# Two pieces of TensorE work put ahead of the scores, and two pieces of VectorE work put ahead of their neighbours

## The chip, the core and the metric

The kernel runs on one core of a Trainium2 chip. Its metric is device time in microseconds (us). Before the change: 723.44 us, the median of three runs (723.38 to 723.95).

## The reference

What is computed, shortened (B = 64 batches of S = 32 rows, D = 256; context of 257 rows of 192; 16 heads of 16; 8 experts):

```python
# 1. cross attention with a residual
xn = layernorm(x);  q = xn @ Wq;  k = ctx @ Wk;  v = ctx @ Wv        # 16 heads of 16
attn = softmax(q k^T / 4 + mask) over the 257 context rows
x  = x + (attn v) @ Wo
# 2. local attention, window of 2 rows to each side, with a residual
xn = layernorm(x);  Q = xn@Wq2+bq;  K = xn@Wk2+bk;  V = xn@Wv2+bv
x  = x + softmax(Q K^T / 16 inside the window) V
# 3. a top-1 router over 8 experts, three layers each, with a residual
xn = layernorm(x);  e = argmax(xn @ Wr + br)
h = gelu(xn@W1[e]+b1[e]);  h = gelu(h@W2[e]+b2[e]);  x = x + h@W3[e]+b3[e]
```

## The kernel before, in words

**Stages.** The first 409 us compute the two attentions and the router's logits, the rest routes the 2048 rows to slots of 128 and runs the experts. The change lies in the attention stage alone.

**Tiles and steps.** A tile T is 128 rows, four batches of 32; there are 16 tiles. Each engine (TensorE, VectorE, ScalarE, GpSimd and the DMA queue SP) has a program of its own, an iteration over T in which k runs from 0 to 3. One pair (T, k), a *step*, is one batch of cross attention, n = 4T + k, and a part of the work on finished tiles. Iterations T = -1, 0, 1 and 14, 15 are written out, 2 to 13 are a hardware loop, and a `last_tile()` closes the stage. The order of each engine's work is the order of its program: nothing overtakes. The engines meet only at semaphores, which are waited for as counts.

**TensorE in one step** (names used below, with the lines of the kernel): **scores** (L1442, function `scores`) of batch n into four banks `ps_s`; **weigh** (L1456), the probabilities of batch n-1 times its values into `ps_o`; **keys** (L1423) of batch n+1 into `ps_kv`; the **first turn** (L1470, `transpose_probs(n, 0)`), the first 128 columns of the probabilities transposed in four pieces into `ps_p`, each piece after ScalarE's exponentials of it; **values** (L1431) of batch n+1, after ScalarE has copied the keys out of `ps_kv` (L819); the **second turn** (L1470 again, `transpose_probs(n, 1)`) into the same bank `ps_p`, for which VectorE must have copied the first turn out (`p_copied[0]`). So the second turn waits for VectorE's copy in every step.

**Between them stands the work on older tiles**, all of it through one bank, `ps_m`, whose users take turns by the semaphores `m_filled` and `m_emptied` (functions `turn` and `my_turn`). At k = 0 the next rows are turned (L1515) and the queries made (L1524). At k = 1 the **output product** (L1579, `end(T, 1)`): `attnT` times Wo for tile T-1; and the local probabilities times their values for tile T-2 (L1487). At k = 2 the **turn of rows** (L1494, `middle(T, 2)`), which transposes `xn2`, the normalised rows of tile T-1; then queries and keys of local attention (L1583). At k = 3 local scores (L1505) and local values (L1497).

**VectorE in one step.** The **masks** (L1040): four instructions, one for each bank of scores, which add the mask, write `prob` and give the row's minimum, the exponential's bias. Then, by k: at k = 1 the **residual** x2 (L1149) and its statistics (L1024, L1027, function `add_input`); `finish_batch` (L1050, L1053, L1057) for batch n-1, whose last instruction writes `attn`; at k = 1 the local result x3 (L1111, L1084); the **copy of the probabilities** (L1062, `copy_probT`, 128x512), which releases the second turn; and `end(T, k)`. In `end(T, 0)` the tile's attention is turned (L1157) and the last context row's value is added (L1160), which gives `attnT`, the operand of the output product at k = 1. In `end(T, 1)` the statistics of x3 are taken (`moments_of(2, ...)`, L1024 and L1027), and x2 is normalised into `xn2` (`normalise(1, ...)`, L1031), the operand of the turn of rows at k = 2.

**ScalarE and GpSimd.** ScalarE makes the four exponentials (L815), copies keys and values out of `ps_kv` (L819, L823), rounds the context (L810) and copies the second turn out (L827). GpSimd keeps the last probability (L657), makes each 1/sqrt(variance) (L663, L665), splits the context into two parts (`split_ctx`, L644, 128x512, both inputs in SBUF), places the queries (L649), and shifts the context (`shift_ctx`, L637, 128x512).

Of the kernel before, what the change touches and what calls it, by code (L numbers as in the profile page):

```python
# [20 lines left out]
def perceiver_kernel(nc, x, ctx_turned, last_turned, mask, Wq, Wk, Wv, Wo, lWq_turned, lbq, lWk_turned, lbk, lWv, lWv_turned, lbv,  # L21
# [32 lines left out]
    with ExitStack() as stack:  # L54
# [103 lines left out]
        x2 = passing("x2", [P, D])  # L158
        x2_kept = passing("x2_kept", [P, D])
        xn2 = sb("xn2", [P, D])  # L160
# [240 lines left out]
        def in_tiles(T):  # L401
            return not isinstance(T, int) or 0 <= T < TILES
# [609 lines left out]
        def _(dve):  # L1012
# [140 lines left out]
            def end(T, k):  # L1153
                has_q, has_out, has_local = parts(T)
                if k == 0 and has_out:
                    dve.wait_ge(o_done, BT * T)
                    d.transpose(attn_turned[:, :, :, :].rearrange("p b c s -> p (b c s)"),  # L1157
                                attn[:, :, :].rearrange("p b d -> p (b d)")).then_inc(attn_turned_done, 1)
                    dve.wait_ge(attn_turned_done, T)
                    d.tensor_tensor(attnT[:, :, :].rearrange("p c (b s) -> p c b s", b=BT),  # L1160
                                    attn_turned[:, :, :, :].rearrange("p b c s -> p c b s"),
                                    last_vT[:, :, bass.ds(BT * (T - 1), BT)].unsqueeze(3).to_broadcast([P, 2, BT, S]),
                                    ALU.add).then_inc(attnT_done, 1)
                if k == 1 and has_local:
                    dve.wait_ge(x3_done, T - 1)
                    moments_of(2, T - 2, x3n[:, 0:D])
                if k == 1 and has_out:
                    normalise(1, T - 1, x2[:, :], xn2[:, :], xn2_done)
                if k == 2 and has_out:
                    dve.wait_ge(m_filled, turn(T, 5) + 1)  # L1170
                    d.tensor_tensor(lqk[:, 0:2, :], ps_m[:, 0:2 * P].rearrange("p (w s) -> p w s", w=2),
                                    lq_bias[:, :].unsqueeze(2).to_broadcast([P, 2, P]), ALU.add).then_inc(m_emptied, 1)
                if k == 3 and has_out:
                    dve.wait_ge(band_done, T)
                    alone(dve)
                    mask_local_scores(ps_m[:, 3 * P:3 * P + S]).then_inc(m_emptied, 1)
# [7 lines left out]
            def iteration(T):  # L1184
                has_q, has_out, has_local = parts(T)
                first = isinstance(T, int) and T < 0
                if first:
                    dve.wait_ge(x_in, 16)
                    moments_of(0, 0, xt[:, :])
                    dve.wait_ge(mask_bytes_in, 16)  # L1190
                    d.tensor_scalar(mask_rows[:, :], mask_bytes[:, :], 1.0, -MASKED, ALU.subtract, ALU.mult).then_inc(mask_done, 1)
                    normalise(0, 0, xt[:, :], xn1[:, :], xn1_done)
                    dve.wait_ge(wk_rounded, 1)
                    split_first_rows(0, wk_split)
                    middle(T, 0)
                    split_last_rows(0, wk_split)
                    dve.wait_ge(wv_rounded, 1)
                    split_first_rows(1, wv_split)
                    split_last_rows(1, wv_split)
                    return  # L1200
                for k in range(BT):
                    n = BT * T + k
                    opening = isinstance(T, int) and T == 0 and k == 0
                    if opening:
                        dve.wait_ge(x_in, 32)
                        moments_of(0, 1, xt[:, :])
                    if k == 1 and has_local:
                        dve.wait_ge(lexp_done, T - 1)
                        d.reciprocal(lrow_inv[:, :], lrow_sum[:, :]).then_inc(linv_done, 1)
                    at = 3 if opening else 2  # L1210
                    if in_tiles(T):
                        mask_scores(T, n, k, range(at))
                    if k == 2:
                        middle(T, k)
                    if opening:
                        normalise(0, 1, xt[:, :], xn1[:, :], xn1_done)
                    if in_tiles(T):
                        mask_scores(T, n, k, range(at, GROUPS))
                    if k == 0:
                        middle(T, k)  # L1220
                    if k == 2 and has_local:
                        normalise(2, T - 2, x3n[:, 0:D], x3n[:, D:2 * D], xn3_done)
                        scale_logits(T - 2).then_inc(logits_done, 1)
                    if k == 1 and has_out:
                        add_input(T)
                    if k == 1 and isinstance(T, int) and T == 1:
                        fuse_router()
                    if isinstance(T, int) and T == 0 and k == 0:
                        last_rows()
                    if not first and exists(T, k - 1) and not (isinstance(T, int) and BT * T + k > B):  # L1230
                        finish_batch(T if k else T - 1, (k - 1) % BT)
                    if k == 3 and next_rows(T):
                        dve.wait_ge(x_in, 16 * (T + 3))
                        moments_of(0, T + 2, xt[:, :])
                    if k % 2:
                        middle(T, k)
                    if in_tiles(T):
                        copy_probT(n)
                    if k == 3 and next_rows(T):
                        normalise(0, T + 2, xt[:, :], xn1[:, :], xn1_done)  # L1240
                    end(T, k)
                    if isinstance(T, int) and T == 0 and k >= 2:
                        fuse_local_weights(k)

# [136 lines left out]
            k = 0  # L1381
# [32 lines left out]
        def _(pe):  # L1414
# [181 lines left out]
            def iteration(T):  # L1596
# [13 lines left out]
                for k in range(BT):  # L1610
                    n = BT * T + k
                    ahead = in_tiles(T) and exists(T, k + 1)
                    has_q, has_out, has_local = parts(T)
                    if in_tiles(T):
                        scores(n, k)
                    if k == 0 and has_q and not (isinstance(T, int) and T == 0):
                        turn_next_rows(T)
                    opening = isinstance(T, int) and T == 0
                    if opening and k in (1, 2):
                        fuse_weights(k - 1)  # L1620
                    if opening and k == 3:
                        fuse_bias(0, 1, 0)
                    if k == 1:
                        end(T, k)
                    if k == 2:
                        middle(T, k)
                    if isinstance(T, int) and T == 0 and k == 0:
                        pe.wait_ge(wv_split, 2)
                        values(0, 0)
                        last_rows()  # L1630
                    if isinstance(T, int) and T == 0 and k == 1:
                        pe.wait_ge(last_copied, 1)
                    if k == 3 and has_out:
                        my_turn(T, 6)
                        local_scores(ps_m[:, 3 * P:3 * P + S]).then_inc(m_filled, 1)
                    if exists(T, k - 1) and not (isinstance(T, int) and BT * T + k > B):
                        weigh(T if k else T - 1, (k - 1) % BT)
                    if ahead:
                        keys(n + 1, (k + 1) % 2)
                    if k == 0 and isinstance(T, int) and T == 0:  # L1640
                        turn_next_rows(T)
                    if k % 2:
                        middle(T, k)
                    if k == 1 and isinstance(T, int) and T == 1:
                        fuse_router()
                    if k == 2:
                        end(T, k)
                    if opening and k == 3:
                        fuse_bias(2, 0, 2)
                        fuse_biases()  # L1650
                    if in_tiles(T):
                        transpose_probs(n, 0)
                    if k == 0 and has_q:
                        queries(T)
                    if ahead:
                        values(n + 1, (k + 1) % 2)
                    if in_tiles(T):
                        transpose_probs(n, 1)
# [254 lines left out]
```

## Time and profile before

| what | value |
|---|---|
| runs | 723.38, 723.44, 723.95 us |
| the profiled execution | 723.63 us, span of its instructions 721.9 us |
| TensorE (matmul) busy | 695.3 us, 96% of the span |
| TensorE weight load busy | 586.4 us, 81% |
| VectorE, ScalarE, GpSimd busy | 469.1 us, 451.1 us, 425.4 us |
| granted TensorE clock over the span | 0.986 of full speed |
| attention stage, 180 to 220 us | TensorE 40.00 of 40 us, VectorE 27.86, ScalarE 26.77, GpSimd 24.30; clock 1.00 |

A matmul's busy time runs until its modelled end, which overlaps the next one's start, so 40.00 of 40 us does not say that nothing waits. The weight loads (PEld in the rows) don't overlap each other, and their starts are the better clock of TensorE's progress. Idle time is in square brackets behind a row, with what ended it; "issue" is a gap that no semaphore explains. Within the loop a tile takes 24.5 us, again and again the same to a few hundredths.

### The profile page before, as it was taken

The numbers are of one execution on the slowest core, as the hardware profiler recorded it, in microseconds if no ns is written. First come the engines' busy times: TensorE is split into PE (matmuls) and PEld (weight loads), VectorE is DVE, ScalarE is ACT, GpSimd is POOL, SyncE is SP. The second block draws the span as 40 slices with busy tenths as digits, with TensorE's granted clock in tenths as the row PEclk, the third lists the DMA queues.
The fourth block names the chain that finished last, engine by engine and source line by source line (L and its number), as shares of the span: only waits on it lengthen the run. The fifth ranks groups of instructions, "written<-read, shape, count | busy, mean of one in ns | idle before, by whom it ended". The sixth has DMA issues, their size and how long they took to land.

```text
span 721.9 us, 26603 instructions
## 1 busy us (share of the span) xinstructions
PE 695.3 (96%) x9305; PEld 586.4 (81%) x9306; DVE 469.1 (65%) x1416; ACT 451.1 (62%) x1073; POOL 425.4 (59%) x578
## 2 busy tenths in 40 slices
PE   8999999999999999999999848999999999999996
PEld 7888888888888888888888737888888888888885
DVE  4466777777777766777777669999952990268000
ACT  4656666666666666666666344575756666575754
POOL 6476565656565656556665114677766676767553
PEclk9999999999999999999999978999999999999999
DMA  7433233322333343434322904239033531271000
GB/s 213 113 86 83 68 82 97 88 80 75 97 92 80 80 95 82 93 80 95 88 80 79 372 31 161 96 98 316 23 103 117 190 118 45 83 237 58 30 7 1
DMA packets 55985, 74.21 MB, mean 103 GB/s; under 512 B 6557, under 2 KB 41662, under 8 KB 55936
## 3 DMA queue, kind: packets, MB, share of 16 engines
q1 hardware_dynamic: 49792, 60.63, 29.7%
q0 software_dynamic: 2944, 8.13, 3.5%
q10 hardware_dynamic: 3200, 4.80, 1.8%
q8 instruction: 30, 0.49, 0.3%
q14 instruction: 19, 0.16, 0.1%
HBM read 67.17 MB, written 7.27 MB: 103 GB/s over the span
## 4 chain that ended last, share of the span: by engine, by line
PE 91%; DVE 3%; ACT 2%; issue 1%; POOL 1%; DMA 1%; SPq 0%; POOLq 0%; ACTq 0%; DVEq 0%
PE ps_s L1788 18%; PE ps_kv L1423 12%; PE ps_kv L1431 11%; PE ps_p L1470 8%; PE ps_o L1456 6%; PE ps_s L1442 6%; PE ps_o L1802 4%; PE ps_p L1736 4%; PE ps_kv L1736 4%; PE ps_s L1768 3%; PE ps_m L1579 2%; PE ps_m L1524 2%; PE ps_m L1583 2%; PE ps_m L1497 2%; PE ps_s L1796 1%
## 5 line engine op out<-in xcount | busy, mean ns | idle before, releaser
L1040 DVE CUSTOM_DVE_ANT_0 prob<-ps_s,mask_add 128x257 f32<-128x257 f32 x256 | 94.8, 422 | 73.9 <-PE ps_s L1442 73.9
L815 ACT ACTIVATE prob<-prob,neg_max 128x257 f32<-128x257 f32 x256 | 111.2, 500 | 43.9 <-DVE neg_max L1040 42.2
L1396 DVE TENSOR_TENSOR w<-w_raw,w 128x512 fp32r<-128x512 f32 x112 | 106.4, 953 | 3.7
L1393 DVE CAST w<-w_raw 128x512 fp32r<-128x512 f32 x94 | 66.2, 705 | 58.9 <-DMA w_raw<-in_L_ffn_W_dram 58.9
L644 POOL TENSOR_TENSOR ctx_parts<-ctx_raw,ctx_parts 128x512 fp32r<-128x512 f32 x64 | 82.8, 1294 | 24.7 <-ACT ctx_parts L810 22.9
L1788 PE MATMUL ps_s<-w,h_hi 128*128 x368 | 91.6, 400 | 1.2 <-ACT h_hi L946 0.8
L1431 PE MATMUL ps_kv<-wkv_hi,ctx_parts 128*128 128x256 f32 x512 | 84.6, 293 | 0.6 <-ACT kT L819 0.5
L1423 PE MATMUL ps_kv<-ctx_parts,wkv_hi 128*128 128x256 f32 x512 | 84.2, 292 | 0.2 <-POOL ctx_parts L644 0.2
L1788 PEld LDWEIGHTS ps_s<-w,h_hi 128*128 128x128 f32 x368 | 67.5, 187 | 18.9 <-issue 4.2
L657 POOL COPY last_prob<-prob 128x4 f32<-128x4 f32 x64 | 12.1, 189 | 119.0 <-ACT prob L815 112.6
L1470 PE MATMUL ps_p<-ident,prob 128*128 128x128 f32 x512 | 80.6, 276 | 1.2 <-DVE probT L1062 1.1
L823 ACT COPY v<-ps_kv 128x512 f32<-128x512 f32 x64 | 37.5, 587 | 70.4 <-PE ps_kv L1431 70.4
L752 POOL TENSOR_TENSOR h_lo<-h,h_hi 128x512 fp32r<-128x512 f32 x46 | 63.3, 1377 | 25.7 <-ACT h_hi L933 21.0
L1423 PEld LDWEIGHTS ps_kv<-ctx_parts,wkv_hi 128*128 128x128 f32 x512 | 69.2, 189 | 2.6 <-issue 0.4
L1431 PEld LDWEIGHTS ps_kv<-wkv_hi,ctx_parts 128*128 128x128 f32 x512 | 69.5, 190 | 2.1 <-ACT kT L819 1.3
L637 POOL TENSOR_TENSOR ctx_raw<-ctx_raw,last_ctxT 128x512 f32<-128x512 f32 x64 | 69.6, 1087 | 1.2 <-DMA ctx_raw<-in_ctx_turned_dram 1.2
L1470 PEld LDWEIGHTS ps_p<-ident,prob 128*128 128x128 f32 x512 | 60.3, 141 | 9.3 <-ACT prob L815 3.3
L920 ACT COPY lqk<-ps_s 128x512 f32<-128x512 f32 x23 | 13.5, 587 | 74.3 <-PE ps_s L1788 74.3
L1062 DVE COPY probT<-ps_p 128x512 f32<-128x512 f32 x64 | 43.9, 686 | 16.4 <-PE ps_p L1470 15.5
L929 ACT ACTIVATE h<-ps_s,bias_cols 128x128 f32<-128x128 f32 x176 | 50.2, 368 | 4.7 <-issue 3.8
L1456 PEld LDWEIGHTS ps_o<-v,probT 128*32 128x32 f32 x4096 | 41.4, 110 | 12.0 <-issue 12.0
L756 POOL TENSOR_TENSOR h_lo<-x3n,h_hi 128x512 fp32r<-128x512 f32 x22 | 30.5, 1385 | 32.0 <-ACT h_hi L969 32.0
(250 smaller groups left out, 1503.1 us busy)
## 6 DMA issues: line engine op xcount, KB each, us to landing
w_raw<-in_L_ffn_W_dram SPq DMA_DIRECT2D x24, 1024.0 KB, 7.3
ctx_raw<-in_ctx_turned_dram SPq DMA_DIRECT2D x63, 256.0 KB, 3.4
mask_add<-mask_dram SPq DMA_DIRECT2D x64, 128.5 KB, 3.3
rows_dram<-x3n ACTq DMA_DIRECT2D x16, 256.0 KB, 4.3
w_raw<-in_L_ffn_W_dram SPq DMA_DIRECT2D x8, 512.0 KB, 3.5
xt<-in_x_dram SPq DMA_DIRECT2D x16, 128.0 KB, 2.0
xr<-in_x_dram SPq DMA_DIRECT2D x16, 128.0 KB, 2.3
slot_x<-rows_dram,slot_ids POOLq DMA_INDIRECT x23, 4.0
```

Of the source, the lines that this page charges most:

```text
L637: g.tensor_tensor(ctx_raw[:, b, :, :], ctx_raw[:, b, :, :], last_ctxT[:, :, bass.ds(n, 1)].to_broadcast([P, 2, JM]), ALU.subtract).then_in ...
L644: g.tensor_tensor(ctx_parts[:, b % 2, 2:4, :], ctx_raw[:, b, :, :], ctx_parts[:, b % 2, 0:2, :].bitcast(F32), ALU.subtract).then_inc(split ...
L752: g.tensor_tensor(h1_parts[LO][:, fs, :], h1[:, fs, :], h1_parts[HI][:, fs, :].bitcast(F32), ALU.subtract).then_inc(h1_done, 1)
L815: a.activation(prob[:, g, :], prob[:, g, :], ACT.Exp, bias=neg_max[:, g:g + 1], scale=-1.0).then_inc(exp_done, 1)
L1040: d.tensor_tensor_reduce(prob[:, r, :], ps_s[r][:, 0:J], mask_add[:, k, :], -(HD ** -0.5), 3.0e38, ALU.add, ALU.min, neg_max[:, r:r + 1]). ...
L1393: d.tensor_copy(w[:, b, HI, part], raw[:, b, part]).then_inc(rounded, 1)
L1396: last = d.tensor_tensor(w[:, b, LO, part], raw[:, b, part], f32(w[:, b, HI, part]), ALU.subtract)
L1423: last = t.matmul(ps_kv[:, half * JM:(half + 1) * JM], w[:, 0, r, half * P:(half + 1) * P], ctx_parts[:, buffer, c, :], start=(i == 0), st ...
L1431: last = t.matmul(ps_kv[:, jt * D:(jt + 1) * D], ctx_parts[:, buffer, c, jt * P:(jt + 1) * P], w[:, 1, r, :], start=(i == 0), stop=(i == 4))
L1456: last = t.matmul(ps_o[h * S:(h + 1) * S, g * BLOCK:(g + 1) * BLOCK], probT[:, jt, g * P + h * S:g * P + (h + 1) * S], v[:, k % 2, jt, g / ...
L1470: last = t.transpose(ps_p[:, g * P:(g + 1) * P], prob[:, g, jt * P:(jt + 1) * P], ident[:, :])
L1788: last = t.matmul(ps_z2[:, :], h1_parts[hp][:, f, :], weight(w2, (2 * e + half) % RING, wp, f % 4 * F2, F2), start=(hp == HI and wp == HI ...
```

## The change

No instruction is added or removed. Four pieces are put elsewhere in their engine's order:

- TensorE: the output product (k = 1) and the turn of rows (k = 2) go ahead of the scores of the same step.
- VectorE: `end(T, 0)`, which turns the attention and makes `attnT`, goes ahead of the copy of the probabilities at k = 0.
- VectorE: in `end(T, 1)` the normalisation of x2 goes ahead of the statistics of x3.

```diff
@@ VectorE, end(T, k)
+                if k == 1 and has_out:
+                    normalise(1, T - 1, x2[:, :], xn2[:, :], xn2_done)
                 if k == 1 and has_local:
                     dve.wait_ge(x3_done, T - 1)
                     moments_of(2, T - 2, x3n[:, 0:D])
-                if k == 1 and has_out:
-                    normalise(1, T - 1, x2[:, :], xn2[:, :], xn2_done)
@@ VectorE, iteration(T)
                     if k % 2:
                         middle(T, k)
+                    if k == 0:
+                        end(T, k)
                     if in_tiles(T):
                         copy_probT(n)
                     if k == 3 and next_rows(T):
                         normalise(0, T + 2, xt[:, :], xn1[:, :], xn1_done)
-                    end(T, k)
+                    if k:
+                        end(T, k)
@@ TensorE, iteration(T)
                     has_q, has_out, has_local = parts(T)
+                    if k == 1:
+                        end(T, k)
+                    if k == 2:
+                        middle(T, k)
                     if in_tiles(T):
                         scores(n, k)
...
-                    if k == 1:
-                        end(T, k)
-                    if k == 2:
-                        middle(T, k)
```

## Rows read from the trace of the kernel before

**Rows 1.** The page: the chain that ended last, by engine.
```profile
PE 91%; DVE 3%; ACT 2%; issue 1%; POOL 1%; DMA 1%; SPq 0%; POOLq 0%; ACTq 0%; DVEq 0%
```

**Rows 2.** Timeline, weight loads, T = 8, k = 1, 2: start, duration (us), engine, line, operation.
```profile
193.77 0.46 PEld L1470 LDWEIGHTS ps_p<-ident,prob 128*128 128x128 f32 x4
194.40 0.23 PEld L1442 LDWEIGHTS ps_s<-kT,qd 32*64 32x64 f32 x16 [0.17 <-issue]
195.02 0.73 PEld L1579 LDWEIGHTS ps_m<-wo,attnT 128*128 128x128 f32 x4 [0.39 <-issue]
196.08 0.64 PEld L1456 LDWEIGHTS ps_o<-v,probT 128*32 128x32 f32 x64 [0.33 <-issue]
...
200.18 0.42 PEld L1470 LDWEIGHTS ps_p<-ident,prob 128*128 128x128 f32 x4
200.77 0.23 PEld L1442 LDWEIGHTS ps_s<-kT,qd 32*64 32x64 f32 x16 [0.17 <-issue]
201.39 0.20 PEld L1494 LDWEIGHTS ps_m<-ident,xn 128*128 128x128 f32 x2 [0.39 <-issue]
201.76 0.64 PEld L1456 LDWEIGHTS ps_o<-v,probT 128*32 128x32 f32 x64 [0.17 <-issue]
...
206.18 0.46 PEld L1470 LDWEIGHTS ps_p<-ident,prob 128*128 128x128 f32 x4
```

**Rows 3.** Timeline, VectorE, the same tile, k = 1.
```profile
195.38 0.43 DVE L1040 CUSTOM_DVE_ANT_0 prob<-ps_s,mask_add 128x257 f32<-128x257 f32 x1 [1.12 <-PE ps_s L1442]
...
198.37 0.22 DVE L1057 TENSOR_TENSOR attn<-ps_o,row_inv 128x64 f32<-128x64 f32 x1
198.92 0.48 DVE L1111 SCALAR_TENSOR_TENSOR x3n<-ps_m,lrow_inv,x_kept 128x256 f32<-128x256 f32 x1 [0.32 <-PE ps_m L1487]
...
199.45 0.68 DVE L1062 COPY probT<-ps_p 128x512 f32<-128x512 f32 x1
...
200.71 0.38 DVE L1031 TENSOR_SCALAR xn<-x,moments,rstd 128x256 f32<-128x256 f32 x1
```

**Rows 4.** Timeline, weight loads, T = 1, k = 1: the second turn.
```profile
52.89 0.42 PEld L1470 LDWEIGHTS ps_p<-ident,prob 128*128 128x128 f32 x4 [0.52 <-DVE probT L1062]
```

**Rows 5.** Timeline, GpSimd, T = 8, k = 1: the split of the context.
```profile
199.42 1.29 POOL L644 TENSOR_TENSOR ctx_parts<-ctx_raw,ctx_parts 128x512 fp32r<-128x512 f32 x1
```

**Rows 6.** Timelines of VectorE and GpSimd, T = 1, k = 1.
```profile
52.75 0.81 DVE L1031 TENSOR_SCALAR xn<-x,moments,rstd 128x256 f32<-128x256 f32 x1
...
52.37 1.04 POOL L637 TENSOR_TENSOR ctx_raw<-ctx_raw,last_ctxT 128x512 f32<-128x512 f32 x1
```

**Rows 7.** Timelines, T = 9, k = 0: VectorE, GpSimd, weight load.
```profile
216.21 0.22 DVE L1057 TENSOR_TENSOR attn<-ps_o,row_inv 128x64 f32<-128x64 f32 x1
...
217.10 0.44 DVE L1157 STREAM_TRANSPOSE attn_turned<-attn 128x256 f32<-128x256 f32 x1
217.67 1.05 DVE L1160 TENSOR_TENSOR attnT<-attn_turned,last_vT 128x256 f32<-128x256 f32 x1
...
217.14 1.29 POOL L644 TENSOR_TENSOR ctx_parts<-ctx_raw,ctx_parts 128x512 fp32r<-128x512 f32 x1 [0.64 <-ACT ctx_parts L810]
...
218.29 0.47 PEld L1470 LDWEIGHTS ps_p<-ident,prob 128*128 128x128 f32 x4
```

**Rows 8.** Timeline, VectorE, after the loop, GpSimd idle: the same L1160.
```profile
409.90 0.43 DVE L1160 TENSOR_TENSOR attnT<-attn_turned,last_vT 128x256 f32<-128x256 f32 x1
```

**Rows 9.** Timelines of VectorE and GpSimd, expert stage.
```profile
494.10 0.69 DVE L1396 TENSOR_TENSOR w<-w_raw,w 128x512 fp32r<-128x512 f32 x1
...
494.20 1.75 POOL L756 TENSOR_TENSOR h_lo<-x3n,h_hi 128x512 fp32r<-128x512 f32 x1 [1.48 <-ACT h_hi L969]
```

**Rows 10.** Timeline, weight loads, T = 15, k = 0: scores, values, second turn.
```profile
384.05 0.23 PEld L1442 LDWEIGHTS ps_s<-kT,qd 32*64 32x64 f32 x16 [0.17 <-issue]
...
387.74 0.54 PEld L1431 LDWEIGHTS ps_kv<-wkv_hi,ctx_parts 128*128 128x128 f32 x4 [0.33 <-ACT kT L819]
...
388.94 0.47 PEld L1470 LDWEIGHTS ps_p<-ident,prob 128*128 128x128 f32 x4
```

## The prediction, made before the changed kernel was run

> **What bounds the kernel now.** I read the page's chain first, then the timeline of TensorE's weight loads over one tile of the loop, then VectorE's and GpSimd's timelines beside it. The chain lies 91% on TensorE [rows 1], so what counts is when TensorE starts its next piece. I measure in starts of weight loads and use three points: the second turn, the scores, and the second turn of the next step. A tile repeats every 24.52 us (second turn of k = 0 at 193.77, the next tile's at 218.29 [rows 2, 7]).
>
> At k = 1 the scores start 0.63 us after the second turn of k = 0, and the second turn of k = 1 starts 5.78 us after the scores (194.40 to 200.18 [rows 2]): 6.41 us. At k = 2 it is 0.59 and 5.41, together 6.00 us [rows 2]. The reader is to see two things there. First, TensorE loses time between pieces of different shape: 0.17 us ahead of the scores, 0.39 behind them, 0.33 between the output product and weigh, 0.17 between the turn of rows and weigh [rows 2]. Second, the second turn of k = 1 started at 200.18, when VectorE's copy of the probabilities ended at 199.45 + 0.68 = 200.13 [rows 3]. VectorE is already level with TensorE in that step. In tile 1 it is plainly late: TensorE's load sat 0.52 us for that copy [rows 4].
>
> **The change part by part.** No instruction is added, so all prices are waits and gaps.
>
> *Output product ahead of the scores (k = 1).* On TensorE alone this saves a gap. The second turn takes 0.63 - 0.17 = 0.46 until the next load. The product then takes what it took up to weigh, 1.06 us with its gap (195.02 to 196.08 [rows 2]); no row shows it ahead of the scores, and I take the same. So the scores start 1.52 us after the second turn of k = 0, not 0.63. Behind them TensorE has 5.78 - 1.06 = 4.72 us of work. But VectorE's work between the scores and its copy has not shrunk. Before, masks started 0.98 us after the scores (195.38) and the copy 5.05 after them (199.45). In between VectorE was idle only 0.32 us, ahead of x3, for the local product [rows 3]. That wait goes, since the local product now stands 1.06 us nearer to the scores. The rest stays: masks, residual, statistics, `finish_batch`, x3. The copy starts at 5.05 - 0.32 = 4.73, ends at 5.41, and the second turn starts 0.05 later, at 5.46. TensorE waits 5.46 - 4.72 = 0.74 us for it. The step becomes 1.52 + 5.46 = 6.98 against 6.41: **+0.57 us**. This is firm: its bounds are +0.5 and +0.7, from the product at 1.0 to 1.2 us.
>
> *Normalisation of x2 ahead of the statistics.* It is needed by the turn of rows, which now stands right behind the second turn of k = 1 instead of behind the scores. Before, it started at 200.71, 6.31 us after the scores of k = 1 [rows 2, 3], when GpSimd's split of the context had just ended (199.42 + 1.29 = 200.71 [rows 5]), and took 0.38 us. Now it follows the copy, at 5.3 to 5.41 after the scores. GpSimd's split stands at 5.02 to 6.31 after the scores; it hangs on exponentials and residual statistics, which don't move against the scores. What an overlap costs is in tile 1: the same normalisation, started at 52.75 inside GpSimd's shift (52.37 to 53.41), took 0.81 us, ending 0.15 after it [rows 6]. So I end it at 6.31 + 0.15 = 6.46 and start the turn of rows at 6.51. TensorE would be there at 5.46 + 0.42 = 5.88: it waits 0.63 us. Bounds: 0 if the overlap costs nothing, 0.63 if it is a full block; I take the block, since the tile 1 row is the same instruction.
>
> The Trainium skill, "SBUF — State Buffer", section "SBUF: two separate sides", calls the SBUF port pair that VectorE and GpSimd share an exclusive lock, which whichever starts first holds for its whole instruction. Shared bandwidth instead would stretch the normalisation only by a part, and the sum would be some 5 us lower; by that rule it is the full 0.63. The tile 1 row agrees with the lock.
>
> *Turn of rows ahead of the scores (k = 2).* From the second turn to the turn of rows: 1.05 (6.51 - 5.46). From there to the scores: 0.20 for the loads and a gap of 0.17 as it had up to weigh [rows 2], 0.37. From scores to second turn: 5.41 less the 0.37 of the turn of rows, 5.04; ScalarE's copy of the keys then holds the values a little. In tile 15 at k = 0, with nothing between scores and keys but weigh, values started 3.69 after the scores and sat 0.33 for that copy [rows 10]; here the copy comes later by the turned rows' copy between the masks, and I take 0.07. The step is 1.05 + 0.37 + 5.04 + 0.07 = 6.53 against 6.00: **+0.53 us**, of which -0.10 is what the move itself gives. VectorE's statistics of x3 end some 0.7 us later against the scores of k = 1, 0.7 us before the next masks. GpSimd's inverse root and shift behind them are as late; ScalarE rounds that context a step later, and nothing is queued behind them sooner. SP's loads wait for masks and splits of the tile before.
>
> *attnT ahead of the copy (k = 0).* Before, the copy stood between `attn` and the turn L1157 at 217.10, and the second turn at 218.29 came some 1.1 us after it [rows 7]: slack. Now the turn (L1157) starts at 216.21 + 0.22 + 0.03 = 216.46, and the addition 0.57 later (217.10 to 217.67), at 217.03. GpSimd's split starts at 217.14. In the kernel before the addition lay inside the split and took 1.05 us, ending 0.29 after it; alone it takes 0.43 [rows 7, 8]. When VectorE starts first, even 0.10 us ahead, it keeps its own time (0.69) and GpSimd's instruction is the longer one, 1.75 [rows 9] against 1.29. So by 0.11 us the addition is first and ends at 217.46, the copy (0.68 [rows 3]) at 218.14 at the latest, before 218.29: **0**. Bounds: 0, and if the split is first, addition to 218.43 + 0.29 = 218.72, copy to 219.40 at the latest, second turn by 219.4: +1.1. I take 0, as nearest to the rows, but 0.11 us is thin.
>
> **The sum.** Per tile 0.57 + 0.53 = 1.10 us. Tiles 2 to 14 have all of it: 13 x 1.10 = 14.3. Tile 15 has the same parts, with VectorE's copy a little later already: 1.0. Tile 1 has no x3, and its second turn, already late by VectorE [rows 4], gains what the product costs: 0.1. Together +15.4 us. Tail and expert stage don't change. Made against the profiled execution's own 723.63 (span 721.9 and 1.7 around it) this is 739.0; the median of the runs is 0.19 lower, so **738.8 us**.
>
> **The rivals.**
> - *The split wins the race at k = 0.* For it: the margin of 0.11 us, and a loop's register arithmetic that could delay the turn. Against it: every row of the loop repeats to some hundredths. The eleven tiles 3 to 13 would lose 1.1 each, +12.1: 750.9 us.
> - *The overlap of the normalisation costs nothing.* Then k = 2 gives -0.10 and a tile +0.47: 14 x 0.47 + 0.1, 730.2 us. Tile 1 speaks against it.
> - *TensorE alone sets the time, and the saved gaps come out: faster.* The place is the second turn of k = 1. It needs VectorE's copy to end some 0.7 us sooner after the scores than 5.41. Then k = 1 would be 1.52 + 4.72 = 6.24 (-0.17), k = 2 -0.17 too, and 14 tiles give -4.8: 718.8 us. With ScalarE's copy of the keys as the floor (4.89 from scores to second turn [rows 10]) it is 1.52 + 4.89 = 6.41, no gain, and -0.10 at k = 2: 722.0 us. It decides where VectorE's work from the masks to the copy is under 4.72 - 0.98 - 0.05 = 3.69 us; it is 4.43. Only an order in which other VectorE work is taken from between them could do that, and the change takes none at k = 1.
> - *No change*: the waits vanish because both engines move together. Against it: the order closes a loop, scores to copy to second turn, whose length I read, not assumed.
>
> **How the numbers follow.** Forecast 0.60, race lost 0.24 (all or some of the tiles), free normalisation 0.08, faster 0.03, no change 0.02, others slower 0.03. Faster by over 0.2% (0.2% is about what can be told from no change here) 0.03, within 0.2% 0.02, slower 0.95. The range goes from 731 to 752: it takes in the lost race and nearly the free normalisation.
>
> **What would show it.** After the change, at k = 1 of a loop tile: scores 1.5 us after the second turn; the second turn 5.46 after the scores with an idle time of some 0.7 put down to VectorE's L1062; the turn of rows 1.05 behind it, its idle time put down to L1031, and that normalisation at about 1.1 us instead of 0.38. At k = 0 L1160 at 0.43 us and the split over 1.4; if L1160 shows over 1.6 us, the race was lost. The tile's period should be 25.6 us, the second turn of k = 3 and its step (5.9 us) as before. If the second turn of k = 1 shows no wait for L1062, the prediction is wrong at its root.

## The result, and the profile after

| | before | after |
|---|---|---|
| median of five runs | 723.44 us (723.17 to 723.95) | 738.39 us (736.59 to 739.40) |
| profiled execution, its span | 723.63, 721.9 us | 739.4, 737.7 us |
| granted clock over the span | 0.986 | 0.984 |

The changed kernel is slower: the ratio is 1.0203 (95% interval 1.0192 to 1.0214). The forecast was 738.8 us.

The page's chain by engine, which had TensorE alone at 91% [rows 1]:

```profile
PE 79%; DVE 7%; ACT 5%; issue 4%; POOL 2%; DMA 1%; DVEq 0%; ACTq 0%; POOLq 0%; SPq 0%
```

The chain now leaves TensorE for a fifth of the span. Where, the timeline of weight loads in tile 8 shows, k = 1 and k = 2 (start, duration, engine, line, operation, idle before). These lines answer to [rows 2]; TensorE's line numbers are 3 higher.

```profile
200.00 0.46 PEld L1473 LDWEIGHTS ps_p<-ident,prob 128*128 128x128 f32 x4
200.43 0.73 PEld L1582 LDWEIGHTS ps_m<-wo,attnT 128*128 128x128 f32 x4
201.49 0.23 PEld L1445 LDWEIGHTS ps_s<-kT,qd 32*64 32x64 f32 x16 [0.33 <-issue]
202.11 0.64 PEld L1459 LDWEIGHTS ps_o<-v,probT 128*32 128x32 f32 x64 [0.39 <-issue]
...
204.33 0.30 PEld L1490 LDWEIGHTS ps_m<-lv,turned 128*128 128x128 f32 x2 [0.29 <-DVE x L1149]
...
207.08 0.42 PEld L1473 LDWEIGHTS ps_p<-ident,prob 128*128 128x128 f32 x4 [0.60 <-DVE probT L1062]
207.90 0.20 PEld L1497 LDWEIGHTS ps_m<-ident,xn 128*128 128x128 f32 x2 [0.40 <-issue]
208.26 0.23 PEld L1445 LDWEIGHTS ps_s<-kT,qd 32*64 32x64 f32 x16 [0.17 <-issue]
...
213.36 0.46 PEld L1473 LDWEIGHTS ps_p<-ident,prob 128*128 128x128 f32 x4
```

The product and its 0.33 us gap do stand ahead of the scores, which now start 1.49 us after the second turn. The gap that is saved is the 0.17 us that stood behind the second turn: the product follows it at once. (It starts 0.03 us before the second turn's loads end, so loads of neighbouring groups do overlap by some hundredths in these rows; no start is moved by that.) But the second turn at 207.08 sat 0.60 us for VectorE's copy (206.34 + 0.68 = 207.02, below), 5.59 us after the scores. Then the turn of rows came 0.82 us behind the second turn. Of that, the second turn's four loads take 0.42, and the other 0.40 is a gap put down to "issue". What held the turn of rows was its operand, as VectorE's and GpSimd's timelines show (they answer to [rows 3, 5, 7]):

```profile
198.76 0.43 DVE L1160 TENSOR_TENSOR attnT<-attn_turned,last_vT 128x256 f32<-128x256 f32 x1
...
202.47 0.43 DVE L1040 CUSTOM_DVE_ANT_0 prob<-ps_s,mask_add 128x257 f32<-128x257 f32 x1 [2.62 <-PE ps_s L1445]
...
205.47 0.22 DVE L1057 TENSOR_TENSOR attn<-ps_o,row_inv 128x64 f32<-128x64 f32 x1
205.81 0.48 DVE L1111 SCALAR_TENSOR_TENSOR x3n<-ps_m,lrow_inv,x_kept 128x256 f32<-128x256 f32 x1
...
206.34 0.68 DVE L1062 COPY probT<-ps_p 128x512 f32<-128x512 f32 x1
206.94 0.84 DVE L1031 TENSOR_SCALAR xn<-x,moments,rstd 128x256 f32<-128x256 f32 x1
...
198.85 1.49 POOL L644 TENSOR_TENSOR ctx_parts<-ctx_raw,ctx_parts 128x512 fp32r<-128x512 f32 x1 [0.64 <-ACT ctx_parts L810]
...
206.35 1.27 POOL L644 TENSOR_TENSOR ctx_parts<-ctx_raw,ctx_parts 128x512 fp32r<-128x512 f32 x1
```

Two meetings of VectorE and GpSimd stand here, with opposite ends. At k = 0 the addition (198.76) starts 0.09 us ahead of the split: it keeps its 0.43 us, and the split takes 1.49 instead of 1.29. At k = 1 the normalisation starts 0.59 us inside the split: it takes 0.84 instead of 0.38, and ends 0.16 us after it (207.78 against 207.62). The addition took 0.43 us in all 16 tiles, where it took 1.05 us in the loop before [rows 7]. In 12 of the tiles the split begins during it, 0.09 to 0.17 us behind its start. In 14 tiles the normalisation meets the split, and it ends 0.15 us after it each time, whether it started 0.50 or 0.88 us inside. The group of L1160, with the durations in ns as min/median/max:

```profile
L1160 DVE TENSOR_TENSOR attnT<-attn_turned,last_vT x16: 426/428/429, 43.4 to 424.8; 128x256 f32<-128x256 f32 x16
```

The list of waits, 100 to 360 us (us in total, times, longest), shows the three in every tile; the same list of the kernel before has none of them. The second, a wait for the bank `ps_m` that x2 frees, turns out to cost nothing (see the part on the prediction):

```profile
PEld ps_p L1473 <- DVE probT L1062: 6.7, 11, 0.6
...
PEld ps_m L1490 <- DVE x L1149: 3.2, 11, 0.3
...
PE ps_m L1497 <- DVE xn L1031: 1.9, 10, 0.2
```

Laid out by steps, from one second turn to the next, in a tile in the middle of the loop (us; the last column is their sum, the tile's period; the experiments' kernels are described below):

| kernel | k = 1 | k = 2 | k = 3 | k = 0 | tile |
|---|---|---|---|---|---|
| before | 6.41 | 6.00 | 5.89 | 6.22 | 24.52 |
| after | 7.08 | 6.28 | 5.89 | 6.23 | 25.48 |
| predicted | 6.98 | 6.53 | as before | as before | 25.6 |
| product only (e3) | 7.08 | 5.99 | 5.89 | 6.23 | 25.19 |
| turn of rows only (e4) | 6.43 | 6.25 | 5.89 | 6.22 | 24.78 |
| TensorE only (e1) | 7.18 | 6.48 | 5.90 | 6.22 | 25.78 |
| split held (e6) | 7.08 | 5.90 | 5.90 | 6.22 | 25.10 |
| sum first (e7) | 6.63 | 6.49 | 5.89 | 6.24 | 25.24 |
| residual first (e5) | 6.48 | 5.94 | 5.90 | 6.24 | 24.56 |
| turn of rows, split held (e8) | 6.43 | 5.91 | 5.89 | 6.23 | 24.46 |

Over the stage, again in second turns: up to k = 0 of tile 1 +0.12 us, tile 1 +1.18 (26.46 to 27.64), tiles 2 to 14 +12.77 (317.71 to 330.48), tile 15 +0.87. That is +14.94 us at the last second turn; the medians differ by 14.95. What follows took 0.8 us more than before in the profiled execution, and in a second execution of the same order (c2, below) 0.7 less, while the runs of the changed kernel spread over 2.8 us: that part is scatter. Up to the last second turn c2 stands at +15.29 us against the kernel before: +0.07, tile 1 +1.01, tiles 2 to 14 +12.78, tile 15 +1.43. So the loop repeats to a hundredth, and the tiles at its ends do not.

### The profile page after: what moved, and what is told of

It reads as the page before. It is cut to its first block, busy times and chain, and to the rows that moved or that the text cites. A ratio compares the mean times of both kernels' runs of the same rounds, so it can differ in the third digit from the quotient of the medians.

```text
span 737.7 us, 26603 instructions
## 1 busy us (share of the span) xinstructions
PE 701.4 (95%) x9305; PEld 589.5 (80%) x9306; DVE 464.5 (63%) x1416; ACT 450.4 (61%) x1073; POOL 427.4 (58%) x578
## 4 chain that ended last, share of the span: by engine, by line
PE 79%; DVE 7%; ACT 5%; issue 4%; POOL 2%; DMA 1%; DVEq 0%; ACTq 0%; POOLq 0%; SPq 0%
PE ps_s L1791 18%; PE ps_kv L1426 9%; PE ps_kv L1434 8%; PE ps_p L1473 6%; PE ps_s L1445 6%; PE ps_o L1459 4%; PE ps_o L1805 4%; PE ps_kv L1739 4%; PE ps_p L1739 4%; ACT prob L815 3%; PE ps_s L1771 2%; PE ps_m L1527 2%; PE ps_m L1586 2%; PE ps_m L1582 2%; PE ps_m L1500 2%
## 5 line engine op out<-in xcount | busy, mean ns | idle before, releaser
L1396 DVE CAST w<-w_raw 128x512 fp32r<-128x512 f32 x94 | 69.3, 737 | 61.3 <-DMA w_raw<-in_L_ffn_W_dram 61.3
L1399 DVE TENSOR_TENSOR w<-w_raw,w 128x512 fp32r<-128x512 f32 x112 | 101.8, 912 | 3.7
L644 POOL TENSOR_TENSOR ctx_parts<-ctx_raw,ctx_parts 128x512 fp32r<-128x512 f32 x64 | 84.8, 1325 | 23.1 <-ACT ctx_parts L810 23.0
L637 POOL TENSOR_TENSOR ctx_raw<-ctx_raw,last_ctxT 128x512 f32<-128x512 f32 x64 | 66.9, 1045 | 1.2 <-DMA ctx_raw<-in_ctx_turned_dram 1.2
L1062 DVE COPY probT<-ps_p 128x512 f32<-128x512 f32 x64 | 43.8, 684 | 9.3 <-PE ps_p L1473 9.2
```

The lines of the kernel that those rows point to most:

```text
L637: g.tensor_tensor(ctx_raw[:, b, :, :], ctx_raw[:, b, :, :], last_ctxT[:, :, bass.ds(n, 1)].to_broadcast([P, 2, JM]), ALU.subtract).then_in ...
L644: g.tensor_tensor(ctx_parts[:, b % 2, 2:4, :], ctx_raw[:, b, :, :], ctx_parts[:, b % 2, 0:2, :].bitcast(F32), ALU.subtract).then_inc(split ...
L1396: d.tensor_copy(w[:, b, HI, part], raw[:, b, part]).then_inc(rounded, 1)
L1399: last = d.tensor_tensor(w[:, b, LO, part], raw[:, b, part], f32(w[:, b, HI, part]), ALU.subtract)
```

## The experiments

The theory: the moved product makes TensorE late for its own scores, VectorE's fixed work from masks to copy then sets the second turn (k = 1), and the moved turn of rows waits for a normalisation that GpSimd's split blocks (k = 2). The rivals: the addition at k = 0 is lost to the split; the moves of VectorE cost the time by themselves; the two TensorE moves cost it, whatever VectorE does; the gap ahead of the turn of rows is TensorE's own and not the operand's.

Every kernel of the experiments has one more register operation in the expert stage. c1 and c2 are the two kernels with nothing else changed. "Ratio" is against runs of the kernel before that were made along with them, with a 95% interval in brackets; "tile" is the period of a loop tile, with a sign the difference to c1. The code is shortened to the lines that matter.

```diff
+                pe.reg_alu(expert_held[q], expert_in[q], 0, ALU.max)
```

**c1_before and c2_after.**

> The kernel before with one register operation more for each expert number TensorE waits by (max with 0), which all kernels of this study carry. It touches the expert stage alone. Expected by all theories: within 1 us of 723.4, the attention stage unchanged.

> The changed kernel with the same register operation. Expected by all theories: within 1.5 us of 738.4; tile period 25.5 us; and, if it belongs to the order and not to chance, again a stretch of granted clock 0.5 near 51 to 54 us.

Measured: c1 724.06 us, ratio 1.0004 (0.9994 to 1.0014), tile 24.51; c2 738.34 us, 1.0198 (1.0181 to 1.0215), tile 25.48. The register operation costs nothing that can be seen, so the others can be read against either kernel. The stretch of low clock near 51 to 54 us did not come back in c2 (last section).

**e1 and e2: one engine's moves alone.** e1 keeps TensorE's two moves and undoes both of VectorE's; e2 is the reverse.

```diff
@@ e1, VectorE
-                    if k == 0:
-                        end(T, k)
                     if in_tiles(T):
                         copy_probT(n)
...
-                    if k:
-                        end(T, k)
+                    end(T, k)
@@ e2, TensorE
-                    if k == 1:
-                        end(T, k)
-                    if k == 2:
-                        middle(T, k)
                     if in_tiles(T):
                         scores(n, k)
```

> Only TensorE's two moves; VectorE's order as before. Theory A (the product ahead of the scores puts the second turn of k = 1 behind VectorE's chain, and the turn of rows waits for a blocked normalisation): k = 1 costs the same 0.67 us as in the changed kernel, the normalisation now stands behind the statistics and ends at scores + 6.5 instead of 6.36, and attnT comes 0.05 late at k = 0, so a tile costs 1.15 us instead of 0.96: 741 us. Rival B (VectorE's own moves cost the time): 723 to 725 us.

> Only VectorE's two moves; TensorE's order as before. Theory A: nothing waits for them there, 723.4 us within 0.7, with L1160 at 0.43 us and the normalisation at about 0.8 us, both off the path. Rival B: 735 us or more.

Measured: e1 743.20 us, ratio 1.0262 (1.0244 to 1.0279), tile +1.27; e2 723.86, 1.0005 (0.9995 to 1.0014), tile 24.50. Weight loads and VectorE of e1:

```profile
207.99 0.42 PEld L1470 LDWEIGHTS ps_p<-ident,prob 128*128 128x128 f32 x4 [0.60 <-DVE probT L1062]
209.01 0.20 PEld L1494 LDWEIGHTS ps_m<-ident,xn 128*128 128x128 f32 x2 [0.60 <-issue]
...
200.18 1.05 DVE L1160 TENSOR_TENSOR attnT<-attn_turned,last_vT 128x256 f32<-128x256 f32 x1
...
208.52 0.38 DVE L1031 TENSOR_SCALAR xn<-x,moments,rstd 128x256 f32<-128x256 f32 x1
```

and VectorE and GpSimd of e2:

```profile
200.12 0.81 DVE L1031 TENSOR_SCALAR xn<-x,moments,rstd 128x256 f32<-128x256 f32 x1
...
199.49 1.29 POOL L644 TENSOR_TENSOR ctx_parts<-ctx_raw,ctx_parts 128x512 fp32r<-128x512 f32 x1
```

The whole loss, and more, comes with TensorE's moves. e1 was expected at +1.15 a tile and 741 us. With VectorE's old order the normalisation is short (0.38) but starts only behind the statistics, as the split ends: the turn of rows comes 1.02 behind the second turn, not 0.82; and the product waits for the addition, blocked again (1.05), which is the other 0.10 of its k = 1. So VectorE's moves make the changed kernel about 5 us faster (743.20 to 738.34), though the normalisation takes twice as long in it. In e2 it is blocked nearly as long (0.81) and costs nothing, since the turn of rows is behind the scores: a blocked instruction is a price only where somebody waits for it.

**e3 and e4: one move of TensorE alone**, each with the move of VectorE that belongs to it (`end(T, 0)` for the product, the normalisation for the turn of rows).

```diff
@@ TensorE                       e3 keeps k == 1 here, e4 keeps k == 2
+                    if k == 1:
+                        end(T, k)
                     if in_tiles(T):
                         scores(n, k)
...
                     if k == 2:
                         middle(T, k)
```

> Of TensorE's moves only the output product's; VectorE's attnT ahead of the copy, the normalisation where it was. Theory A: k = 1 costs 7.08 against 6.41 us, k = 2 nothing: 14 tiles x 0.67 = 9.4, 733 us (734 with the slow stretch of the clock in tile 1). Rival C (most of the cost is the turn of rows waiting): 727 us or less.

> Of TensorE's moves only the turn of rows; the normalisation ahead of the statistics, attnT where it was. Theory A: the copy ends where it did, the normalisation starts inside GpSimd's split and ends 0.15 us after it, so the turn of rows waits 0.3 us instead of 0.4, and k = 2 costs 6.20 against 6.00: 14 x 0.20 = 2.8, 726.4 us. Rival C: 731 us or more.

Measured: e3 734.43 us, 1.0141 (1.0125 to 1.0156), tile +0.68; e4 728.29, 1.0064 (1.0048 to 1.0079), tile +0.27. Together 0.95, against +0.96 for both (25.48 against 24.52): the costs add, each in its own step (table). e4 lies 1.9 us above what was expected, in part since its k = 2 is 6.25 and not 6.20. The second turn of e3 waits as long as with the whole change:

```profile
205.76 0.42 PEld L1473 LDWEIGHTS ps_p<-ident,prob 128*128 128x128 f32 x4 [0.60 <-DVE probT L1062]
```

**e6: is it the split that blocks the normalisation?** In the changed kernel GpSimd's split at k = 1 waits until the normalisation is done; nothing is taken out.

```diff
@@ GpSimd, iteration(T)
+                    if k == 1 and has_out:
+                        pool.wait_ge(xn2_done, T)
                     if in_tiles(T) and exists(T, k + 2):
                         split_ctx(*later(T, k, 2))
```

> The changed kernel with GpSimd's split at k = 1 held back until the normalisation of x2 has ended. If the split blocks the normalisation: it takes 0.38 instead of 0.84 us, the turn of rows follows the second turn without a wait, k = 2 loses 0.40 us: 13 to 14 tiles, 733 us. If the normalisation is slow for another reason: unchanged 738 us, or slower by the added wait.

Measured: 731.98 us, 1.0112 (1.0097 to 1.0128), tile 25.10, which is 0.38 less than c2. VectorE and GpSimd:

```profile
203.21 0.68 DVE L1064 COPY probT<-ps_p 128x512 f32<-128x512 f32 x1
203.80 0.41 DVE L1033 TENSOR_SCALAR xn<-x,moments,rstd 128x256 f32<-128x256 f32 x1
...
204.37 1.27 POOL L644 TENSOR_TENSOR ctx_parts<-ctx_raw,ctx_parts 128x512 fp32r<-128x512 f32 x1 [1.10 <-DVE xn L1033]
```

The split starts later and nobody misses it; the normalisation is back at 0.41, k = 2 at 5.90, which is 0.10 under the kernel before. So the "issue" gap ahead of the turn of rows was its operand's, and the move of the turn of rows by itself is a gain of the size that the prediction gave it (-0.10). The hold removes the k = 2 loss entirely and leaves the k = 1 loss untouched (7.08).

**e5 and e7: less VectorE work between masks and copy.** The faster rival said that the k = 1 wait goes where VectorE's work from masks to copy shrinks. With the product ahead of the scores, x2 can be made ahead of the masks too. e5 moves the sum and its per-row statistics (the aggregate stays behind the masks), e7 only the sum.

```diff
@@ VectorE, iteration(T)
+                    if k == 1 and has_out:
+                        add_input(T)        # e5: x2, bn_stats.  e7: x2
                     if in_tiles(T):
                         mask_scores(n, k)
...
-                    if k == 1 and has_out:
-                        add_input(T)
+                    if k == 1 and has_out:
+                        join_input(T)       # e5: bn_aggr.  e7: bn_stats, bn_aggr
```

> The changed kernel with the residual x2 and its bn_stats ahead of the masks at k = 1 (possible only there, since the product is ready before the scores), bn_aggr behind the masks. Theory A: 1 us of VectorE's work leaves the chain from masks to copy; the second turn starts 4.9 us after the scores, held by ScalarE's copy of the keys, and the normalisation starts before GpSimd's split: tile 24.4 us, 721.8 us, faster than before. Rival B or D (the cost is TensorE's own, by shapes or clock): 736 to 738 us.

> The changed kernel with only the residual sum x2 ahead of the masks at k = 1, its statistics behind them as before. In the kernel with both ahead the masks came 0.11 us late and ScalarE's copy of the keys set the step. Theory A: masks at scores + 0.98 again, VectorE's copy ends at 4.83, level with the keys' copy, second turn at 4.89; k = 1 is 6.39, k = 2 5.94, tile 24.43 against 24.51 us: 722.6 us, 1 us under before, at the edge of what can be told.

Measured: e5 724.08 us, 1.0008 (0.9999 to 1.0017), tile 24.56: the loss is gone, but the gain expected is not there. e7 733.52, 1.0131 (1.0115 to 1.0147), tile 25.24: a clear miss, by 11 us. Weight loads, VectorE and GpSimd of e5:

```profile
195.51 0.23 PEld L1452 LDWEIGHTS ps_s<-kT,qd 32*64 32x64 f32 x16 [0.33 <-issue]
...
199.30 0.53 PEld L1441 LDWEIGHTS ps_kv<-wkv_hi,ctx_parts 128*128 128x128 f32 x4 [0.33 <-ACT kT L819]
...
200.49 0.46 PEld L1480 LDWEIGHTS ps_p<-ident,prob 128*128 128x128 f32 x4
200.93 0.25 PEld L1504 LDWEIGHTS ps_m<-ident,xn 128*128 128x128 f32 x2
...
200.12 0.41 DVE L1031 TENSOR_SCALAR xn<-x,moments,rstd 128x256 f32<-128x256 f32 x1
...
200.23 1.43 POOL L644 TENSOR_TENSOR ctx_parts<-ctx_raw,ctx_parts 128x512 fp32r<-128x512 f32 x1
```

and of e7:

```profile
204.09 0.42 PEld L1477 LDWEIGHTS ps_p<-ident,prob 128*128 128x128 f32 x4 [0.19 <-DVE probT L1062]
205.11 0.20 PEld L1501 LDWEIGHTS ps_m<-ident,xn 128*128 128x128 f32 x2 [0.60 <-issue]
...
202.48 0.22 DVE L1057 TENSOR_TENSOR attn<-ps_o,row_inv 128x64 f32<-128x64 f32 x1
202.82 0.48 DVE L1111 SCALAR_TENSOR_TENSOR x3n<-ps_m,lrow_inv,x_kept 128x256 f32<-128x256 f32 x1
...
203.95 1.04 DVE L1031 TENSOR_SCALAR xn<-x,moments,rstd 128x256 f32<-128x256 f32 x1
...
203.57 1.27 POOL L644 TENSOR_TENSOR ctx_parts<-ctx_raw,ctx_parts 128x512 fp32r<-128x512 f32 x1
```

In e5 the second turn no longer waits for VectorE. It comes 4.98 us after the scores, since the values now sit 0.33 us for ScalarE's copy of the keys: that floor had been put at 4.89 in the prediction's faster rival, and it eats what the saved gap gives (k = 1: 6.48 against 6.41). The 0.09 between 4.98 and 4.89 goes with the masks, which start 1.09 us behind the scores instead of 0.98, held by the work now ahead of them. In e7 the wait for VectorE is still there (0.19), and the split starts 0.38 us ahead of the normalisation; in e5 it was 0.11 us behind it. GpSimd's split stands nearly still against the scores (4.72 and 4.62 us after them), VectorE's normalisation does not (4.61 and 5.00), by about the 0.42 us of statistics that e7 leaves between masks and copy. This turns 0.41 us into 1.04, and k = 2 from 5.94 into 6.49. The expectation for e7 had left out this meeting, though the prediction had priced it. It was wrong at k = 1 too: 6.63 against 6.39 expected, as the copy ended 5.08 us after the scores and not 4.83.

**e9 and e10: what a lost race at k = 0 would have cost.** The same extra instruction of 0.45 us (one more turn of the attention, into columns that are overwritten later) stands ahead of the addition in e9 and behind it in e10.

```diff
@@ VectorE, end(T, 0)
+                    d.transpose(lqk[:, 2:4, :], attn)   # e9
                     d.transpose(attn_turned, attn)      # L1157
                     d.tensor_tensor(attnT, attn_turned, last_vT)   # L1160
+                    d.transpose(lqk[:, 2:4, :], attn)   # e10
```

> The changed kernel with one more 32x32-block turn of attn into an unused place, ahead of L1157 at k = 0: 0.36 to 0.45 us of VectorE. Race theory (whoever starts first holds the port): the addition L1160 now starts inside the split and ends 0.29 us after it, over 1 us instead of 0.43, and the second turn of k = 0 is 1.1 us later: tile 26.6 us, about 753 us. If there is no such block: the copy is only 0.4 us later than it was, tile 25.7 us, 741 us, as in the next kernel.

> The same additional turn behind the addition L1160 instead of ahead of it. The addition still starts ahead of the split: 0.43 us; the copy ends 0.36 to 0.45 us later, some 0.2 us past its slack: tile 25.7 us, 741 us, by both theories.

Measured: e9 750.10 us, 1.0361 (1.0341 to 1.0381), tile 26.42; e10 737.52, 1.0187 (1.0168 to 1.0206), tile 25.50. The addition in e9:

```profile
L1162 DVE TENSOR_TENSOR attnT<-attn_turned,last_vT x16: 426/1349/1414, 43.6 to 436.3; 128x256 f32<-128x256 f32 x16
```

and in e10:

```profile
L1160 DVE TENSOR_TENSOR attnT<-attn_turned,last_vT x16: 426/428/429, 43.2 to 423.8; 128x256 f32<-128x256 f32 x16
```

Same work, 12.6 us apart; by second turns 11.1 of them lie in tiles 2 to 14 and 1.0 in tile 1, where a second race went the other way (last section). Both kernels came out some 3 us below what was expected (753 and 741). In e10 the extra instruction is all but free (a tile takes 0.02 more), since the slack before the second turn hides it: that slack had been taken for 0.2 us too small. In e9 the addition starts 0.22 us behind the split and ends 0.28 us after it: 0.92 us a tile. The rival's 750.9 us was the right price for the event (with 750.1 measured here, though with an instruction more); it just doesn't happen in the changed kernel, where VectorE is first by 0.09 us in every tile of the loop.

**e8: the good part alone.** The turn of rows ahead of the scores, the normalisation ahead of the statistics, and e6's hold on the split; the product and `end(T, 0)` stay where they were before.

> Only the turn of rows ahead of the scores and the normalisation ahead of the statistics, and GpSimd's split at k = 1 held back until that normalisation has ended. Theory A: k = 1 as before, no wait at k = 2, which costs 5.94 against 6.00 us: tile 24.45, 722.6 to 723.5 us, and 5 us less than without the hold. If the wait at k = 2 is not the port: 728 us.

Measured: 722.60 us (721.97 to 724.14), 0.9982 (0.9973 to 0.9991), tile 24.46. Weight loads, VectorE and GpSimd:

```profile
199.91 0.42 PEld L1472 LDWEIGHTS ps_p<-ident,prob 128*128 128x128 f32 x4
200.30 0.25 PEld L1496 LDWEIGHTS ps_m<-ident,xn 128*128 128x128 f32 x2
200.72 0.23 PEld L1444 LDWEIGHTS ps_s<-kT,qd 32*64 32x64 f32 x16 [0.17 <-issue]
...
199.78 0.41 DVE L1033 TENSOR_SCALAR xn<-x,moments,rstd 128x256 f32<-128x256 f32 x1
...
200.34 1.27 POOL L644 TENSOR_TENSOR ctx_parts<-ctx_raw,ctx_parts 128x512 fp32r<-128x512 f32 x1 [1.32 <-DVE xn L1033]
```

It is the only order that beats both kernels. The gain, 0.18% or 1.3 us against the kernel before, is no larger than what I called the least that can be told; the interval leaves 1 out, and the trace has it where it should be, at k = 2 (5.91 against 6.00). Up to the last second turn the trace is 0.8 us ahead of that of the kernel before. e4, the same order without the hold on the split, took 728.29 us: the hold alone is worth 5.7 us, which shows the cause at k = 2 a second time. The loads of the turn of rows follow those of the second turn with no gap.

## Why the prediction was right, step by step

- **The mechanism at k = 1 was right and mis-sized by 0.10.** Scores 1.49 us after the second turn (1.52 predicted); second turn 5.59 after the scores (5.46), with the idle time on L1062 (0.60). The mis-sized term is "the copy starts at 5.05 - 0.32": it takes all of the idle time ahead of x3 for a wait for the local product. x3 started 4.32 us after the scores, 4.52 before, not 4.20: between the end of `attn` (205.47 + 0.22 = 205.69) and x3 (205.81) 0.12 us stayed. The local product did not hold it. Where x3 waits for it, x3 starts 1.00 us after its load (197.92 to 198.92 before, and 1.00 in e5 too), and here it was 1.48 (204.33 to 205.81). In e7, where the local product is loaded without a wait, the same 0.12 stands (202.70 to 202.82). What it consists of stays open. One wait the prediction did not have at all: the local product sits 0.29 us for its bank `ps_m`, which x2 (L1149) frees, and x2 is no nearer to the scores than before. It costs nothing, as TensorE idles another 0.60 us behind it: together 0.89, where 0.74 + 0.13 = 0.87 would be due. e3 repeats the price of the step alone (0.67).
- **At k = 2 the mechanism was right and the size half.** 0.28 measured, 0.53 predicted; the term is "it waits 0.63 us". The turn of rows came 0.82 behind the second turn, not 1.05, because the split stood 4.86 to 6.13 after the scores, not 5.02 to 6.31. I had kept it fixed to the scores. But before, it waited for ScalarE's rounding of the context, which ended 4.94 after the scores; in the changed kernel it ended at 4.15, and the split began right behind GpSimd's instruction before it (206.21 + 0.19). So the normalisation ended 6.29 after the scores, 0.17 sooner than predicted; the second turn was 0.13 later, and the load started 0.12 us behind the operand instead of 0.05: 0.17 + 0.13 - 0.07 is the 0.23. The block itself was read rightly: the normalisation ended 0.16 after the split, 0.15 in the row used [rows 6]. e6 shows the cause by removing it. The exclusive lock of the Trainium skill ("SBUF — State Buffer", section "SBUF: two separate sides") says that the one who starts first holds the ports for its whole instruction; the traces agree at each meeting of the loop read here, from a start 0.63 us behind GpSimd's (e2) to one 0.09 ahead of it. In tile 1 the recorded starts do not settle who is first (last section).
- **k = 0, k = 3: zero, as said.** The margin in the race is 0.09 us (0.11 predicted), the addition 0.43, the split 1.49. e9 gives 0.92 us a tile for the other outcome, 1.1 predicted.
- **Tile 1 was wrong: 1.18 us, 0.1 predicted.** In tile 1 the second turn gained what the product costs, as said (in c2 +0.23 us at k = 1), but the turn of rows then waited for a normalisation that was blocked longer than any in the loop (in c2 k = 2 took 6.75 us against 5.97). Of the 1.18 us, 0.17 go with the low clock that c2 did not have. The prediction used the 0.81 us of [rows 6] for the loop and not for the tile it stands in. GpSimd and VectorE of the changed kernel:

```profile
52.49 0.76 POOL L649 TENSOR_TENSOR qd<-q,head_mask 128x128 f32<-128x128 f32 x2
53.20 1.05 POOL L637 TENSOR_TENSOR ctx_raw<-ctx_raw,last_ctxT 128x512 f32<-128x512 f32 x1
...
53.10 1.30 DVE L1031 TENSOR_SCALAR xn<-x,moments,rstd 128x256 f32<-128x256 f32 x1
```

- **The sum** was right within 0.4 us partly by luck, since terms offset each other: tiles 2 to 14 gave 12.77 against 14.3, tile 15 0.87 against 1.0, tile 1 1.18 against 0.1. By steps alone I was 0.14 us too high in each loop tile.
- **The rivals.** The race was not lost, though by 0.09 us, and its chance of 0.24 was not too large for such a margin: 0.45 us of work ahead of the addition is enough. The free normalisation fell (e6: freeing it gives 6.4 us). The faster rival needed less VectorE work between masks and copy, and e5 reached that: its cheaper version, with the keys' copy as the floor, came nearly true (no loss, no gain), and its 718.8 us (by its own terms 718.7) is closed by that floor. Whether an earlier keys' copy would release the rest wasn't tried.

## What to carry to other kernels

Where two engines are level, a move that saves a gap on one can lengthen the loop through the other: work out the loop (scores, masks, copy, second turn) with every operand and bank that the moved piece shares. Do not take the whole idle time shown ahead of an instruction as what goes when its releaser comes sooner: of the 0.32 us ahead of x3, 0.12 stayed. Where VectorE and GpSimd both read SBUF, find each pair of instructions that meet within a few tenths of a microsecond and price both orders, since a move on either engine shifts the other's start too; one wait on the engine with slack can settle the order for good (e6, e8).

## What the hardware showed that was not expected

- **A recorded start ahead of GpSimd's does not always win.** In tile 1 of the changed kernel the normalisation started 0.10 us before the shift L637, and still ended 0.15 us after it: 1.30 us where 0.38 is its own time. At its start L649 was running too, and ended at 53.25. In c2, e3 and e9 it was the same (0.12, 0.10 and 0.11 us ahead; 1.29 to 1.32 us). But in e1 and e10, also 0.12 us ahead and also with L649 running, the normalisation took 0.40 us, and GpSimd's shift took 1.18 instead of 1.05:

```profile
52.39 0.76 POOL L649 TENSOR_TENSOR qd<-q,head_mask 128x128 f32<-128x128 f32 x2
53.11 1.18 POOL L637 TENSOR_TENSOR ctx_raw<-ctx_raw,last_ctxT 128x512 f32<-128x512 f32 x1
...
52.98 0.40 DVE L1031 TENSOR_SCALAR xn<-x,moments,rstd 128x256 f32<-128x256 f32 x1
```

  So a second race stands in tile 1, decided within some hundredths of a microsecond and worth 0.8 us at k = 2 (6.75 in c2, 5.91 in e1 and e10). What decides it isn't settled by these runs.
- **The granted clock fell in tile 1 in some executions.** From 51 to 54 us the changed kernel's mean was 0.52 of full speed, its lower level of 1.2 GHz; in the 3 us before, TensorE was busy for 2.81. Busy time of each engine, clock, DMA share and GB/s in windows of the changed kernel:

```profile
48.00:51.00 3.00, 2.81 (x26) 2.64 (x25) 2.79 (x12) 2.53 (x6) 0.94 (x3) 1.00 0.12 32
51.00:54.00 3.00, 3.00 (x17) 3.00 (x17) 2.60 (x10) 0.00 (x0) 2.92 (x6) 0.52 0.33 105
```

and of c2, the same order of work:

```profile
51.00:54.00 3.00, 2.53 (x20) 2.08 (x19) 2.61 (x10) 0.71 (x2) 2.94 (x5) 1.00 0.31 102
```

In c2, too, TensorE was busy for 2.81 of the 3 us before, so that does not tell the two apart, and the cause stays open. It fell in e3 and e9 as well (0.53 and 0.54) and not in e1, e6 and e10 (1.00), each with the same 2.81 us before. The kernel before has such a short fall too, elsewhere: 0.52 from 408 to 411 us, behind 3 us in which TensorE was busy for 1.43. The price in tile 1 can be read: from the second turn of k = 0 to that of k = 1 it was 9.06 us with the fall and 8.35 without, but to the turn of rows, which waits for the normalisation, 9.76 and 9.64. Of 0.71 us, 0.12 got past that wait, since the blocked normalisation held the turn of rows in both.
